# Sheaf pass of a four-layer graph kernel: 40 columns fetched by TensorE from a table in four float32r tiles, 12 gathered by GpSimd

## The chip, the core and the metric

One core of one Trainium2 chip. The metric is the device time of one execution in microseconds (us). Engines by their names in the profile: PE is TensorE (PEld its weight loads), DVE is VectorE, ACT is ScalarE, POOL is GpSimd, SP is SyncE.

## The reference

Four graph layers run one after the other over the same graph of N = 12500 nodes and 412500 edges (sorted by destination): attention, relations, sheaf, typed attention. The change touches the sheaf layer alone:

```python
xs, xd = (x[src], x[dst])                       # 16 values for each end of each edge
def reflection(a, b):
    h = relu(concatenate([a, b], axis=1) @ W1.T + b1)
    return h @ W2.T + b2
def householder(v):
    vn = v / maximum(norm(v, axis=1, keepdims=True), 1e-12)
    return eye(d)[None] - 2.0 * vn[:, :, None] * vn[:, None, :]
F_s = householder(reflection(xs, xd)); F_d = householder(reflection(xd, xs))
L_sd = -einsum('eki,ekj->eij', F_s, F_d)
coef = deg_inv_sqrt[src] * deg_inv_sqrt[dst]
msg_s = coef[:, None] * einsum('eij,ej->ei', L_sd, xd)
msg_d = coef[:, None] * einsum('eji,ej->ei', L_sd, xs)
out = relu(x - zeros.at[src].add(msg_s) - zeros.at[dst].add(msg_d))
```

## The kernel before, in words

`sheaf_pass` walks the edges in 62 chunks. A chunk is 52 columns (`J`) of 128 edges, one edge per partition. For each edge it needs the row of its source node: 16 values and the inverse root of the degree, `W` = 17 numbers.

**Two ways to fetch a row.** For the first `SJP` = 16 columns POOL gathers rows from DRAM with one indirect DMA per column (line 2097). For the other `SPE` = 36 columns PE fetches them from a table in SBUF. The node's tile number t (0 to 97) is cut into a low part (t mod 7) and a high part (14 values). DVE builds, for four columns at a time, seven one-hot matrices in bfloat16 (`build_low`, line 2164: seven comparisons of 512 elements). PE multiplies each with the table part of that low value (17 x 14 = 238 columns); the table is held as three bfloat16 parts whose sum is the float32 value, so a column of edges costs 7 x 3 = 21 matmuls that add up in PSUM (`find`, line 2352, two columns at a time, 42 matmuls). DVE then multiplies the 2 x 238 results with a one-hot of the high part (line 2183) and sums over the high part (line 2187); the two are `take`. The one-hot of the high part is made once per chunk (`spread_high`, line 2170).

**The chunk's pipeline.** Every engine runs a `turn` per chunk, of `SN` = 18 steps. In step n of the turn of chunk a:
- PE does `find` of step n for the next chunk, then for chunk a `spin` (a transpose, line 2363, steps 3 to 15), `hide` (first layer of the small network, line 2372, steps 4 to 16), `unhide` (second layer, line 2382, steps 5 to 17), and in steps 9 to 12 `add_alike` for the chunk before a (line 2394: sums over edges with the same source).
- DVE does `take` of step n-1 for the next chunk; in even steps `build_low` for a later group; in step 0 `begin` (lines 2207 to 2218: fills in the destination's values, joins the ends) and `spread_high`; in steps 1 to 7 `reflect`, and in step 8 `sum_by_dst` for the chunk before; in step 14 `find_places` (ends with line 2289, which releases POOL's scatters); from step 9 `compare` (line 2229) and from step 6 `take_v` (line 2222). The last `take_v` of a turn stands after step 17.
- ACT copies and bends between PE's steps, and copies the sums of `add_alike` out (`take_added`, line 2449).

`find` of step n waits for `take` of step n-2 (two result buffers in PSUM) and for the one-hots; `take` waits for `find`; `unhide` waits for the `take_v` before it. So PE and DVE keep pace within a step or two.

**POOL** does for each chunk 52 scatters with addition into DRAM (line 2113), each waiting for the one four before it, and between them (after every third) the gathers for the chunk three further on. A chunk's scatters wait for line 2289 of that chunk; halfway through, it frees the buffer of the chunk before, on which ACT's `take_added` of the chunk after waits. PE, DVE and POOL loop over pairs of chunks; DVE's loop starts at line 2326.

**SP** issues the loads: index, the low parts (line 2073, one buffer per chunk parity), high parts, and edge data. PSUM: `found` has two buffers of one bank each; the transposes, `hidden`, `v`, `added` and a mixed bank take one each.

## Time and profile before

| | us |
|---|---|
| median of 3 runs (27705.8 to 27721.6) | 27713.97 |
| profiled execution, its own time | 27723.67 |
| its span | 27721.6 |
| sheaf pass: first `find` to last scatter | 15751 to 23652 |

| engine | busy us of the whole span | share |
|---|---|---|
| PE | 22581.0 | 81% |
| PEld | 17103.5 | 62% |
| DVE | 19269.3 | 70% |
| ACT | 1534.2 | 6% |
| POOL | 17285.6 | 62% |

A busy share is an average over stages with different limits, and only about 7900 us of the span belong to the changed pass. What matters there is which engine goes without a rest, and, where two engines hand work to each other in steps, which of them ends each step. The idle time of an engine is listed with what ended it.

### The profile page before, as it was taken

The numbers are of one execution on the slowest core, as the hardware profiler recorded it, in microseconds if no ns is written. First come the engines' busy times: TensorE is split into PE (matmuls) and PEld (weight loads), VectorE is DVE, ScalarE is ACT, GpSimd is POOL, SyncE is SP. The second block draws the span as 40 slices with busy tenths as digits, with TensorE's granted clock in tenths as the row PEclk, the third lists the DMA queues.
The fourth block names the chain that finished last, engine by engine and source line by source line (L and its number), as shares of the span: only waits on it lengthen the run. The fifth ranks groups of instructions, "written<-read, shape, count | busy, mean of one in ns | idle before, by whom it ended". The sixth has DMA issues, their size and how long they took to land. (4 is left out here: it accounts for less than half of the span.)

```text
span 27721.6 us, 477560 instructions
## 1 busy us (share of the span) xinstructions
PE 22581.0 (81%) x178452; PEld 17103.5 (62%) x178452; DVE 19269.3 (70%) x45474; ACT 1534.2 (6%) x3291; POOL 17285.6 (62%) x15844
## 2 busy tenths in 40 slices
PE   0788876888857999969999398889898897399996
PEld 0444433444426888858888388888888886155554
DVE  4788885555555777757777376676766765499996
ACT  0000000000000000000000011111111111100000
POOL 1555556666654555546655478888888888455555
PEclk9998987999977999979999699999999998599998
DMA  4222221111111111111111122222222222522221
GB/s 80 61 65 63 62 59 28 40 40 40 40 34 32 33 34 34 34 29 32 32 32 31 19 37 39 35 39 37 37 39 35 39 40 25 132 57 60 60 60 42
DMA packets 1658941, 1225.33 MB, mean 44 GB/s; under 512 B 1258202, under 2 KB 1501076, under 8 KB 1615348
## 3 DMA queue, kind: packets, MB, share of 16 engines
q0 software_dynamic: 870816, 181.33, 10.7%
q1 hardware_dynamic: 676628, 585.00, 7.7%
q10 hardware_dynamic: 110016, 437.07, 4.0%
q8 instruction: 1197, 19.61, 0.3%
q14 instruction: 284, 2.33, 0.0%
HBM read 736.61 MB, written 465.15 MB: 43 GB/s over the span
## 5 line engine op out<-in xcount | busy, mean ns | idle before, releaser
L946 PE MATMUL gat_e_found<-gat_e_parts,gat_e_lowhot 128*128 128x400 bf16 (+1 forms) x30504 | 5867.6, 356 | 1077.8 <-DVE gat_e_rows L915 927.4
L2352 PE MATMUL sheaf_e_found<-sheaf_e_parts,sheaf_e_lowhot 128*128 128x238 bf16 x46872 | 5274.5, 274 | 939.5 <-DVE sheaf_e_lowhot L2164 462.4
L2113 POOL DMA_INDIRECT bysrc<-sheaf_e_toadd,sheaf_e_torow x3224 | 5162.4, 1601 | 1312.5 <-issue 758.2
L1027 POOL DMA_INDIRECT gat_e_rows<-att_t,gat_e_index x4464 | 4236.5, 949 | 2676.6 <-DMA gat_e_rows<-att_t,gat_e_index 1423.3
L2352 PEld LDWEIGHTS sheaf_e_found<-sheaf_e_parts,sheaf_e_lowhot 128*128 128x128 bf16 x46872 | 4688.9, 101 | 1370.0 <-issue 546.2
L750 POOL DMA_INDIRECT rgcn_e_rows<-rel_t,rgcn_e_index x3968 | 3753.8, 946 | 2844.5 <-DMA rgcn_e_rows<-rel_t,rgcn_e_index 1468.4
L946 PEld LDWEIGHTS gat_e_found<-gat_e_parts,gat_e_lowhot 128*128 128x128 bf16 x30504 | 3035.1, 100 | 3909.7 <-DVE gat_e_rows L915 996.3
L1843 PEld LDWEIGHTS rgcn_e_found<-rgcn_e_parts,rgcn_e_lowhot 128*128 128x128 bf16 x52080 | 5033.8, 99 | 559.4 <-issue 490.5
L1843 PE MATMUL rgcn_e_found<-rgcn_e_parts,rgcn_e_lowhot 128*128 128x224 bf16 x52080 | 5245.8, 264 | 78.9 <-issue 72.0
L2801 POOL DMA_INDIRECT typed_e_rows<-typed_t,typed_e_index x1984 | 1903.4, 959 | 1434.7 <-DMA typed_e_rows<-typed_t,typed_e_index 910.5
L946 PE MATMUL typed_e_found<-typed_e_parts,typed_e_lowhot 128*128 128x400 bf16 x14880 | 2686.0, 338 | 57.9 <-DVE typed_e_lowhot L890 57.9
L946 PEld LDWEIGHTS typed_e_found<-typed_e_parts,typed_e_lowhot 128*128 128x128 bf16 x14880 | 1477.8, 99 | 1093.4 <-issue 131.6
L2183 DVE TENSOR_TENSOR sheaf_e_picked<-sheaf_e_found,sheaf_e_highhot 128x476 f32<-128x476 f32 x1116 | 723.7, 648 | 1956.3 <-PE sheaf_e_found L2352 1855.8
L910 DVE TENSOR_TENSOR gat_e_picked<-gat_e_found,gat_e_highhot 128x800 f32<-128x800 f32 (+1 forms) x992 | 1011.4, 1020 | 774.4 <-PE gat_e_found L946 767.6
L1719 DVE TENSOR_TENSOR rgcn_e_bykind<-rgcn_e_kindsp,rgcn_e_hot 128x512 f32<-128x512 f32 x620 | 427.3, 689 | 1374.6 <-PE rgcn_e_kindsp L1863 1373.7
L2097 POOL DMA_INDIRECT sheaf_e_rows<-sheaf_t,sheaf_e_index x992 | 1074.7, 1083 | 390.2 <-issue 290.5
L1696 DVE TENSOR_SCALAR rgcn_e_lowhot<-rgcn_e_low,whole_lowf 128x512 bf16<-128x512 f16 x4340 | 1306.7, 370 | 0.3
L2164 DVE TENSOR_SCALAR sheaf_e_lowhot<-sheaf_e_low,whole_lowf 128x512 bf16<-128x512 f16 x3906 | 1192.8, 375 | 0.3 <-DVE sheaf_e_parts L826 0.2
L699 DVE TENSOR_TENSOR_SCAN gat_e_sums<-gat_e_miscp,gat_e_sums,gat_e_scaled 128x52 f32<-128x52 f32 x4960 | 1134.8, 301 | 0.0
L915 DVE TENSOR_REDUCE gat_e_rows<-gat_e_picked 128x32 f32<-128x800 f32 (+1 forms) x992 | 1026.4, 1035 | 34.0
L2382 PE MATMUL sheaf_e_vp<-sheaf_w,sheaf_e_hidden 128*128 128x32 f32 x6448 | 828.0, 274 | 235.8 <-DVE sheaf_e_v L2222 232.8
L2382 PEld LDWEIGHTS sheaf_e_vp<-sheaf_w,sheaf_e_hidden 128*128 128x128 f32 x6448 | 815.2, 199 | 255.9 <-issue 240.5
(497 smaller groups left out, 22017.0 us busy)
## 6 DMA issues: line engine op xcount, KB each, us to landing
sheaf_e_allsrc<-src_d ACTq DMA_DIRECT2D x62, 1664.0 KB
sumsatt<-gat_e_sums ACTq DMA_DIRECT2D x62, 1404.0 KB
rgcn_e_low<-low_d SPq DMA_DIRECT2D x124, 640.0 KB
typed_e_types<-in_type_t SPq DMA_DIRECT2D x62, 1280.0 KB, 8.1
typed_t<-typed_p_y SPq DMA_DIRECT2D x98, 765.0 KB
gat_e_rows<-att_t,gat_e_index POOLq DMA_INDIRECT x4464
sheaf_e_low<-low_d SPq DMA_DIRECT2D x62, 1152.0 KB
sumsatt<-gat_e_sums ACTq DMA_DIRECT2D x62, 1092.0 KB
```

The lines of the kernel that those rows point to most:

```text
L699: return dve.tensor_tensor_scan(out, keep, values, before, ALU.mult, ALU.add)
L750: pool.indirect_dma_start(self.rows[k][:, j, :], None, table, rows(self.index[k][:, j:j + 1]))\
L946: last = pe.matmul(self.found_ps[n % 2][:, c, 0:self.width * self.cut.highs], hot[:, k, col * P:(col + 1) * P], self.table.column(part, k) ...
L1027: pool.indirect_dma_start(rows_t[a.k][:, j, :], None, table, rows(index[a.k][:, j:j + 1]))\
L1696: last = dve.tensor_scalar(low_hot[(k * NQ + q) % 2][:, n, :], low[k][:, q * QC * P:(q + 1) * QC * P], g.low_f[:, n:n + 1], None, ALU.is_e ...
L1843: last = pe.matmul(found_ps[at % 2][:, c, 0:NHI * FD], low_hot[at % 2][:, n, c * P:(c + 1) * P], short.column(part, n), start=n == 0 and p ...
L2097: pool.indirect_dma_start(rows_t[a.k][:, j, :], None, table, rows(index[a.k][:, j:j + 1]))\
L2113: pool.indirect_dma_start(g.by_src[k][r], rows(to_row[k][:, j:j + 1]), to_add[k][:, j, 0:FD], None, compute_op=ALU.add).then_inc(summed[k] ...
L2164: last = dve.tensor_scalar(hot[:, n, :], low[a.k][:, q * QC * P:(q + 1) * QC * P], g.low_f[:, n:n + 1], None, ALU.is_equal)
L2352: last = pe.matmul(found_ps[n % 2][:, c, 0:W * NHI], hot[:, k, col * P:(col + 1) * P], short.column(part, k), start=part == 0 and k == 0, ...
L2382: last = pe.matmul(v_ps[:, c * F2:(c + 1) * F2], hidden[(a.k * NQ13 + m) % 2][:, c * P:(c + 1) * P], w2, start=True, stop=True)
L2801: pool.indirect_dma_start(rows_t[a.k][:, j, :], None, table, rows(index[a.k][:, j:j + 1]))\
```

## The change

TensorE's share of the columns goes from 36 to 40, and GpSimd's gathers from 16 to 12 per chunk. The tile number is cut by 4 instead of 7: four low values, and 25 high values made up to 26, so a table part is 17 x 26 = 442 columns wide. The table is held in two float32r parts instead of three bfloat16 ones, so a column of edges is 4 x 2 = 8 matmuls; the one-hots of the low part become float32r, those of the high part bfloat16. A turn has 20 steps instead of 18. `found` takes two banks per buffer; to make room `ends` and `added` share a bank, with waits that keep PE's writes and ACT's reads apart, and `add_alike` moves to steps 10 to 13 and ahead of `find`. The last `take_v` comes in step 18. `find_places` moves to step 15. The low parts are loaded in halves of a chunk. The 52 comparisons are spread over 11 steps instead of 9.

```diff
-SPE = 36
+SPE = 40
 SJP = J - SPE
 SG = SPE // QC
 SN = 2 * SG
 NQ13 = J // QC
-CUTS = (0, 12, 24, 36, J)
+PART = J // 4
+CUTS = tuple(range(0, J + 1, PART))
...
+    cut_by = Cut(FLO, FHI + FHI % 2, g.few_low_d, g.few_high_d, 2, F32R)
+    tiles, highs = cut_by.tiles, cut_by.highs
...
-        low = [s.sb(f"low{k}", [P, SPE * P], F16) for k in range(2)]
+        low = [s.sb(f"low{k}", [P, SPE * P // 2], F16) for k in range(2)]
...
-        short = SplitTable(s, sevenths(g), [values[:, :, :]], W, same[0][:, :, :].rearrange("p j q -> p (j q)").bitcast(F32))
-        low_hot = [s.sb(f"lowhot{k}", [P, NLO, QC * P], BF16) for k in range(2)]
-        high_hot = [s.sb(f"highhot{k}", [P, SPE, NHI]) for k in range(2)]
-        picked = s.sb("picked", [P, 2, W, NHI])
+        short = SplitTable(s, cut_by, [values[:, :, :]], W, same[0][:, :, :].rearrange("p j q -> p (j q)").bitcast(F32))
+        low_hot = [s.sb(f"lowhot{k}", [P, tiles, QC * P], cut_by.exact) for k in range(2)]
+        high_hot = [s.sb(f"highhot{k}", [P, SPE, highs], BF16) for k in range(2)]
+        picked = s.sb("picked", [P, 2, W, highs])
...
-        found_ps = [s.ps(f"found{k}", [P, 2, 256]) for k in range(2)]
-        ends_ps, hidden_ps, v_ps = s.ps("endsp", [P, P]), s.ps("hiddenp", [P, QC * P]), s.ps("vp", [P, QC * F2])
-        added_ps, misc_ps = s.ps("addedp", [P, 16, MW]), s.ps("miscp", [P, 512])
+        found_ps = [s.ps(f"found{k}", [P, 2, 512]) for k in range(2)]
+        hidden_ps, v_ps, misc_ps = s.ps("hiddenp", [P, QC * P]), s.ps("vp", [P, QC * F2]), s.ps("miscp", [P, 512])
+        shared_ps = s.ps("sharedp", [P, 512])
+        ends_ps, added_ps = shared_ps[:, 0:P], shared_ps[:, P:P + PART * MW].rearrange("p (j c) -> p j c", c=MW)
...
+                def load_low(a, half, fresh):
+
+                    if not fresh:
+                        sp.wait_ge(low_built, a.c * SG - (SG // 2 if half == 0 else 0))
+                    lo = SJP + half * (SPE // 2)
+                    sp.dma_start(low[half][:, :], line(low_v, a.c, lo * P, (lo + SPE // 2) * P))\
+                        .then_inc(low_in[half], 16)
...
-                    if not fresh:
-                        sp.wait_ge(low_built, (c - 1) * SG)
-                    sp.dma_start(low[k][:, :], line(low_v, c, SJP * P, J * P)).then_inc(low_in[k], 16)
+                    load_low(a, 0, fresh and k == 0)
                     if not fresh:
                         sp.wait_ge(high_built, c - 1)
-                    sp.dma_start(high_in[k][:, :], chunk(g.high_d, i, k)[:, SJP:]).then_inc(high_in_s[k], 16)
+                    sp.dma_start(high_in[k][:, :], chunk(cut_by.high_d, i, k)[:, SJP:]).then_inc(high_in_s[k], 16)
...
+                    load_low(a, 1, fresh and k == 0)
...
-                    if q == 0:
-                        dve.wait_ge(low_in[a.k], a.turn * 16 + 16)
+                    half, at = q // (SG // 2), q % (SG // 2)
+                    if at == 0:
+                        dve.wait_ge(low_in[half], a.c * 16 + 16)
                     if not fresh:
                         dve.wait_ge(found, 2 * (a.c * SG + q) - 2)
                     hot = low_hot[(a.k * SG + q) % 2]
-                    for n in range(NLO):
-                        last = dve.tensor_scalar(hot[:, n, :], low[a.k][:, q * QC * P:(q + 1) * QC * P],
+                    for n in range(tiles):
+                        last = dve.tensor_scalar(hot[:, n, :], low[half][:, at * QC * P:(at + 1) * QC * P],
                                                  g.low_f[:, n:n + 1], None, ALU.is_equal)
...
-                                             g.count_f[:, 0:NHI].unsqueeze(1).to_broadcast([P, SPE, NHI]),
-                                             high_in[a.k][:, :].unsqueeze(2).to_broadcast([P, SPE, NHI]),
+                                             g.count_f[:, 0:highs].unsqueeze(1).to_broadcast([P, SPE, highs]),
+                                             high_in[a.k][:, :].unsqueeze(2).to_broadcast([P, SPE, highs]),
...
-                                             found_ps[n % 2][:, :, 0:W * NHI].rearrange("p c (f h) -> p c f h", f=W),
+                                             found_ps[n % 2][:, :, 0:W * highs].rearrange("p c (f h) -> p c f h", f=W),
                                              high_hot[a.k][:, 2 * n:2 * n + 2, :].unsqueeze(2)
-                                             .to_broadcast([P, 2, W, NHI]), ALU.mult))
+                                             .to_broadcast([P, 2, W, highs]), ALU.mult))
...
-                        if reflects and n == 14:
+                        if reflects and n == 15:
                             find_places(o, old)
                         if moves and n >= 9:
-                            compare(o, a, range((n - 9) * 6, min(J, (n - 8) * 6)))
-                        if moves and n >= 6:
+                            compare(o, a, range((n - 9) * J // (SN - 9), (n - 8) * J // (SN - 9)))
+                        if moves and 6 <= n < 6 + NQ13:
                             take_v(a, n - 6)
-                    if moves:
-                        take_v(a, NQ13 - 1)
...
-                        for part in range(3):
-                            for k in range(NLO):
-                                last = pe.matmul(found_ps[n % 2][:, c, 0:W * NHI], hot[:, k, col * P:(col + 1) * P],
+                        for part in range(cut_by.pieces):
+                            for k in range(tiles):
+                                last = pe.matmul(found_ps[n % 2][:, c, 0:W * highs], hot[:, k, col * P:(col + 1) * P],
                                                  short.column(part, k), start=part == 0 and k == 0,
-                                                 stop=part == 2 and k == NLO - 1)
+                                                 stop=part == cut_by.pieces - 1 and k == tiles - 1)
...
+                def spin(a, m, first=False, beside=False, added_before=None):
                     M = a.c * NQ13 + m
                     if m == 0:
                         pe.wait_ge(ends_ready, a.c + 1)
                     if not (first and m == 0):
                         pe.wait_ge(ends_copied, M)
+                    if beside:
+                        pe.wait_ge(added_out, added_before)
...
-                def add_alike(a, part, first=False):
+                def add_alike(a, part, copied, first=False):
+                    pe.wait_ge(ends_copied, copied)
...
+                        adds = reflects and 10 <= n <= 13
+                        if adds:
+                            copied = a.c * NQ13 + n - 3 if moves else a.c * NQ13
+                            add_alike(old, n - 10, copied, first=isinstance(old.turn, int) and old.c == 0)
                         if fetches:
                             find(nxt, n)
                         if moves and 3 <= n <= 15:
-                            spin(a, n - 3, first)
+                            spin(a, n - 3, first, adds, old.c * 4 + n - 9)
                         if moves and 4 <= n <= 16:
                             hide(a, n - 4, first)
                         if moves and 5 <= n <= 17:
                             unhide(a, n - 5, first)
-                        if reflects and 9 <= n <= 12:
-                            add_alike(old, n - 9, first=isinstance(old.turn, int) and old.c == 0)
...
+                        if reflects and 10 <= n <= 13:
+                            take_added(old, n - 10)
```

`Cut(tiles, highs, low_d, high_d, pieces, exact)` only holds its arguments. `g.few_low_d` and `g.few_high_d` exist already; they are those of the attention layers' cut by four.

## Rows read from the trace of the kernel before

**Rows 1.** Groups in 16370 to 22250 us: engine, tiles, count; busy, mean ns; idle, releasers.
```profile
L2352 PE MATMUL sheaf_e_found<-sheaf_e_parts,sheaf_e_lowhot 128*128 128x238 bf16 x35892 | 4044.2, 274 | 412.3 <-DVE sheaf_e_rows L2187 330.5 <-issue 54.0 <-DVE sheaf_e_lowhot L2164 27.2
L2113 POOL DMA_INDIRECT bysrc<-sheaf_e_toadd,sheaf_e_torow x2465 | 3944.4, 1600 | 879.6 <-issue 573.6 <-DMA bysrc<-sheaf_e_toadd,sheaf_e_torow 302.8 <-DVE sheaf_e_torow L2289 3.3
...
L2164 DVE TENSOR_SCALAR sheaf_e_lowhot<-sheaf_e_low,whole_lowf 128x512 bf16<-128x512 f16 x2996 | 916.8, 375 | 0.0
...
L2187 DVE TENSOR_REDUCE sheaf_e_rows<-sheaf_e_picked 128x34 f32<-128x476 f32 x855 | 554.8, 649 | 29.4
L2183 DVE TENSOR_TENSOR sheaf_e_picked<-sheaf_e_found,sheaf_e_highhot 128x476 f32<-128x476 f32 x855 | 554.4, 648 | 1499.3 <-PE sheaf_e_found L2352 1408.8 <-issue 50.2 <-DVE sheaf_e_highhot L2170 11.6
```

**Rows 2.** The same stretch, busy time of each engine and TensorE's granted clock.
```profile
core 0: us, PE busy (x) PEld busy (x) DVE busy (x) ACT busy (x) POOL busy (x), PEclk, DMA share, GB/s
16370.00:22250.00 5880.00, 5293.14 (x53910) 4941.19 (x53908) 4071.46 (x10747) 850.46 (x1618) 4769.22 (x3223) 0.96 0.29 37
```

**Rows 3.** Timeline of POOL in mid-pass: start, duration, instruction, idle before.
```profile
18018.22 1.55 POOL L2113 DMA_INDIRECT bysrc<-sheaf_e_toadd,sheaf_e_torow  x1 [0.30 <-issue]
18020.07 1.01 POOL L2097 DMA_INDIRECT sheaf_e_rows<-sheaf_t,sheaf_e_index  x1 [0.30 <-issue]
18021.39 1.57 POOL L2113 DMA_INDIRECT bysrc<-sheaf_e_toadd,sheaf_e_torow  x1 [0.30 <-DMA bysrc<-sheaf_e_toadd,sheaf_e_torow]
```

**Rows 4.** Instructions of lines 2289 and 2113: duration, first and last start.
```profile
L2289 DVE TENSOR_SCALAR sheaf_e_torow<-sheaf_e_place,sheaf_e_spare x62: 248/249/450, 16035.5 to 23510.0; 128x52 int32<-128x52 f32 x62
...
L2113 POOL DMA_INDIRECT bysrc<-sheaf_e_toadd,sheaf_e_torow x3224: 1549/1552/3262, 16036.6 to 23650.2; - x190
```

**Rows 5.** Timeline of PE: a step of the turn, with `add_alike`.
```profile
18240.46 4.50 PE L2352 MATMUL sheaf_e_found<-sheaf_e_parts,sheaf_e_lowhot 128*128 128x238 bf16 x42
18244.80 0.27 PE L2363 MATMUL sheaf_e_endsp<-whole_ident,sheaf_e_ends 128*128 128x128 f32 x1
18244.91 1.06 PE L2372 MATMUL sheaf_e_hiddenp<-sheaf_e_endst,sheaf_w 128*128 128x128 f32 x8
18245.80 0.98 PE L2382 MATMUL sheaf_e_vp<-sheaf_w,sheaf_e_hidden 128*128 128x32 f32 x8
18246.61 1.05 PE L2394 MATMUL sheaf_e_addedp<-sheaf_e_piece,sheaf_e_same 128*128 128x18 bf16 x36
18247.52 4.51 PE L2352 MATMUL sheaf_e_found<-sheaf_e_parts,sheaf_e_lowhot 128*128 128x238 bf16 x42
```

**Rows 6.** Timeline of DVE: turn end, step 0, steps 7 and 8.
```profile
18166.23 0.29 DVE L2222 TENSOR_TENSOR sheaf_e_v<-sheaf_e_vp,sheaf_b 128x128 f32<-128x128 f32 x1 [4.22 <-PE sheaf_e_vp L2382]
18171.09 0.65 DVE L2183 TENSOR_TENSOR sheaf_e_picked<-sheaf_e_found,sheaf_e_highhot 128x476 f32<-128x476 f32 x1 [4.57 <-PE sheaf_e_found L2352]
...
18217.65 0.64 DVE L2183 TENSOR_TENSOR sheaf_e_picked<-sheaf_e_found,sheaf_e_highhot 128x476 f32<-128x476 f32 x1
...
18224.94 0.65 DVE L2183 TENSOR_TENSOR sheaf_e_picked<-sheaf_e_found,sheaf_e_highhot 128x476 f32<-128x476 f32 x1 [4.52 <-PE sheaf_e_found L2352]
...
18232.27 0.64 DVE L2183 TENSOR_TENSOR sheaf_e_picked<-sheaf_e_found,sheaf_e_highhot 128x476 f32<-128x476 f32 x1
```

**Rows 7.** Timeline of PE in step 7: after a wait of 3.35 us.
```profile
18217.88 1.05 PE L2382 MATMUL sheaf_e_vp<-sheaf_w,sheaf_e_hidden 128*128 128x32 f32 x8 [3.35 <-DVE sheaf_e_v L2222]
18218.76 6.14 PE L2352 MATMUL sheaf_e_found<-sheaf_e_parts,sheaf_e_lowhot 128*128 128x238 bf16 x42
```

**Rows 8.** Timeline of PE, typed pass: a `find` 400 columns wide.
```profile
25006.08 4.22 PE L946 MATMUL typed_e_found<-typed_e_parts,typed_e_lowhot 128*128 128x400 bf16 x24
```

**Rows 9.** Groups of the whole span with other widths and types.
```profile
L1863 PE MATMUL rgcn_e_kindsp<-rgcn_ws,rgcn_e_hcol 64*128 64x512 f32 x1240 | 752.7, 689 | 1.9 <-DVE rgcn_e_bykind L1719 1.9
...
L915 DVE TENSOR_REDUCE typed_e_hrows<-typed_e_picked 128x32 f32<-128x800 f32 x620 | 611.3, 986 | 21.1
L910 DVE TENSOR_TENSOR typed_e_picked<-typed_e_found,typed_e_highhot 128x800 f32<-128x800 f32 x620 | 609.2, 983 | 243.9 <-PE typed_e_found L946 209.6 <-DVE typed_e_scaled L2844 14.2 <-DVE typed_e_attr L2827 12.8
...
L2710 DVE TENSOR_SCALAR typed_e_typehot<-typed_e_types,whole_lanef 128x512 bf16<-128x512 int32 x310 | 155.9, 503 | 0.3
...
L826 DVE CAST sheaf_e_parts<-sheaf_e_same 128x238 bf16<-128x238 f32 x21 | 14.2, 678 | 0.3
```

More of the change, by code:

```diff
@@ L24 @@
 BF16 = mybir.dt.bfloat16
+F32R = mybir.dt.float32r
 F16 = mybir.dt.float16
@@ L2054, in sheaf_pass @@
         acc = by_edge(sums_d)
-        low_v, all_v = (t.rearrange("(c m) -> c m", m=J * P) for t in (g.low_d, g.src16_d))
+        low_v, all_v = (t.rearrange("(c m) -> c m", m=J * P) for t in (cut_by.low_d, g.src16_d))
         per_table = J // NSUM
@@ L2324, in _ @@
                 turn(o, At(1, 0))
-                base, per = o.n, 2 * 44
+                base, per = o.n, 2 * (SN + 26)
                 with dve.Fori(1, NCH // 2 - 2) as i:
@@ L2349, in find @@
                         col = (n % 2) * 2 + c
-                        for part in range(3):
-                            for k in range(NLO):
-                                last = pe.matmul(found_ps[n % 2][:, c, 0:W * NHI], hot[:, k, col * P:(col + 1) * P],
+                        for part in range(cut_by.pieces):
+                            for k in range(tiles):
+                                last = pe.matmul(found_ps[n % 2][:, c, 0:W * highs], hot[:, k, col * P:(col + 1) * P],
                                                  short.column(part, k), start=part == 0 and k == 0,
-                                                 stop=part == 2 and k == NLO - 1)
+                                                 stop=part == cut_by.pieces - 1 and k == tiles - 1)
                     last.then_inc(found, 1)
-                def spin(a, m, first=False):
+                def spin(a, m, first=False, beside=False, added_before=None):
                     M = a.c * NQ13 + m
@@ L2470, in turn @@
                                 .then_inc(stored[old.k], 16)
-                        if reflects and 9 <= n <= 12:
-                            take_added(old, n - 9)
                 turn(At(0, 0), reflects=False, first=True)
```

## The prediction

> **What bounds the kernel now.** I read the pass in this order: the groups of its steady middle, POOL's timeline, the first and last starts of the two lines that hand POOL its work, and then one turn on PE and on DVE step by step.
>
> *POOL does not rest.* In 5880 us it issues 2465 scatters, 47.4 chunks' worth: 124.0 us per chunk. Its idle time is almost all "issue" and its own earlier scatters; line 2289, which releases it, ends 3.3 us of it [rows 1]. A scatter takes 1.85 us from start to start and a gather 1.32 [rows 3], so 52 and 16 of them would take 96.2 + 21.1 = 117.3 us; the other 6.7 are longer ones (mean 1600 ns where most take 1552) and waits for earlier scatters [rows 1, 4].
>
> *PE and DVE are no faster.* The first scatter starts 1.1 us after the first run of line 2289. The last chunk's 52 scatters must start at 23650.2 - 51 x 1.85 = 23555.9, 46 us after its line 2289 at 23510.0 [rows 4]. So in 61 chunks the pair gained only 46 us on POOL; half of that I count to the last turns, which have few or no finds (an estimate). The pair's own period is within a microsecond of POOL's.
>
> *Who ends which step.* With `add_alike` a PE step is 7.06 us: find 4.34, transpose 0.11, hide 0.89, unhide 0.81, sums 0.91; without, 6.15 [rows 5]. PE sets steps 10 to 16: four with sums (one has 48 matmuls of sums instead of 36, 0.3 longer) and three without, 47.2 us. DVE sets steps 0 to 6: from the `take` at 18171.09 to the one at 18217.65 it goes through 46.6 us of its own work. Step 7 is 7.3 us, in which DVE waits 4.52 for a `find`, and step 8 is 7.3, DVE's own [rows 6]. What remains of 124.0 for step 9 and the turn's end is 15.6; it holds a 4.57 us gap on DVE where its loop starts anew, in every second chunk [rows 6], 2.3 on average. The row puts that gap down to PE; I take it for the loop's own.
>
> **The change, part by part, per chunk.**
>
> *Matmuls of a find.* 42 of 238 columns become 16 of 442. A bfloat16 find of 24 matmuls of 400 columns takes 4.22 less its last one's tail of 0.16: 0.169 each [rows 5, 8], so 0.187 for 442 if float32r streams a column as fast as bfloat16 does, 2.99 us instead of 4.34. The trace has no float32r. The other end is float32: 0.689 us for 512 columns as a mean with its tail, or 752.7/1240 = 0.607 without, twice per product [rows 9], 0.52 for 442. I take the low end: `hide` issues four float32 matmuls and eight run [rows 5], so a float32 product is split in two, and float32r is one; and the row nearest in width and pattern is the 400-column one. PE per chunk: 20 x 2.99 + 13 x 1.81 + 4 x 0.99 = 87 us instead of 18 x 4.34 + 23.5 + 3.9 = 106. Both ends are kept as cases.
>
> *Weight loads.* They now carry four bytes. The 32-column float32 matmuls run at 0.81/8 = 0.101 us, which can only be their weight loads; the 128-column ones at 0.89/8 = 0.111 [rows 5]. Loads in series with the streaming would show as more than 0.2. So they hide under 0.187 us, at no cost; unhidden they would be 16 x 0.101 = 1.6 us per find, the other end. The Trainium skill ("TensorE: Matmul & The Clock Gate", Weight-path perf modes) speaks against this change: it has the fast weight load on for 128 weights only where their type is not FP32. By that rule, the trace agrees: 36 bfloat16 loads and matmuls pass in 0.91 us, 0.025 each, a quarter of 0.101 [rows 5].
>
> *Low one-hots.* 9 groups of 7 comparisons become 10 of 4, written as four bytes. One costs 916.8/2996 = 0.306 us start to start. With a four-byte operand on one side, the same 512 elements have a mean of 503 ns against 375 [rows 1, 9]: 0.434 each, 1.74 us a group instead of 2.14, if DVE keeps its two elements per cycle. The other end is one element per cycle, 0.27 more each (the 128 ns step from four to two is a quarter of 512 cycles, so the next is half), 2.8 a group. I take 1.74: the int32 row is a comparison of the same length with one four-byte side.
>
> *Take.* 2 x 17 x 26 = 884 elements instead of 476. Both halves cost 648 ns now, and at 800 elements 983 and 986 [rows 1, 9], 1.04 ns per element; so 1.07 each, +0.85 us per take, and 20 instead of 18. `spread_high` handles 1040 elements instead of 504, +0.55. DVE in all: 4071/47.4 = 86 us per chunk now [rows 2], less 9 x 2.14 and 18 x 1.30, plus 10 x 1.74, 20 x 2.14 and 0.55: 104.
>
> *The turn.* Steps 0 to 6 hold seven takes and four groups: 46.6 + 6.0 - 1.6 + 0.55 = 51.5. Step 7 waits for unhide and find; that find now takes 1.64 us longer than one of 4.50 [rows 5], after PE had waited 3.35 [rows 7]. I carry the 1.64 over: 1.1 + 2.99 + 1.64 + 0.15 = 5.9. Step 8: 7.3 + 0.85 - 0.4 = 7.8. Steps 10 to 13 are PE's, 4.80 + 0.99 = 5.8 each, 23.2. Steps 14 to 18: PE 4.8, DVE 4.9 and 3.2 in turn, so 4.8 each, 24.0. Step 9 and the end, now steps 9 and 19: a find that may start cold, 5.0, and DVE's 3.3 + 2.3 of loop, since no `take_v` waits there any more: 10.6. Sum 123.0 against 124.0. PE's 19 us are given back by two more steps and by the seven takes that stand where DVE sets the pace.
>
> *POOL.* Four gathers less: 117.3 - 5.3 + 6.7 = 118.7 us. It would wait for line 2289 some 4 us per chunk. *SP.* The low halves are issued behind waits for one-hots already built; half 1 stands behind the wait for `same_ready` and is wanted eight steps later, some 50 us, and the next index load, which queues behind it, is wanted by POOL only 15 steps on. Nothing. *New waits.* `spin` waits for ACT's copy of the sums (0.36 us work), with the 3 us find between; behind it queue hide and unhide. Nothing while the find covers it, otherwise 4 x 0.5 us. *Ends.* The table costs 8 casts instead of 21 (14.2 us now [rows 9]), at most 442/238 as long, and 4 subtractions instead of 14: -8. The first chunk's finds run alone: 18 x 4.34 = 78 against DVE's 20 x 2.15 + 10 x 1.74 = 60: -18. POOL no longer trails by what it had lost up to the last two turns: -23.
>
> *Sum.* 60 x -1.0 - 8 - 18 - 23 = -109 us. The profiled execution took 27723.67 (span 27721.6), 10 above the median of the runs, 27713.97. So 27615 in its terms and 27605 in the median's; I say 27610, 0.4% faster. Its own range, with 1.5 us per chunk either way: 27520 to 27700.
>
> **Rivals.**
>
> 1. *POOL bounds* (faster). PE and DVE overlap better than my steps, and the pass runs at POOL's 118.7: -5.3 x 60 - 49 = -367: 27360 (with 118.7 as its period). For it: DVE's 104 us and PE's 87 are both below. Against: they take turns at setting the pace, and DVE's 51.5 in steps 0 to 6 has no slack.
> 2. *The comparison into float32r runs at one element per cycle* (slower). +1.07 us a group. Five groups stand in steps DVE sets, +5.3; the other five bring DVE's pairs of steps from 8.1 to 9.2 against PE's 9.6, +1.5 by hand-over. +6.8 x 60 = +410: 28020. It decides from +1.8 us per chunk, a comparison of 0.50 instead of 0.43 us. For it: no row writes four bytes from two. Against: the int32 row.
> 3. *float32r streams at half bfloat16's rate* (slower). A find is 5.9 us, PE sets every step: 20 x 5.9 + 27.4 = 145.6, with hand-over 150: +26 x 62 = 29300; at the float32 row's 0.52, past 31000. For it: nothing but the lack of a row.
> 4. *PE drops to half clock in the steps DVE sets* or its weight loads are not hidden (slower). PE would be busy 4.8 of some 7 us there instead of 6.15 of 6.7. At 1.2 GHz a find of 6.0 and 3.6 of the rest make 9.6 against DVE's 6.8, six times: +17 per chunk, 28600. The granted clock is 0.96 of 2.4 GHz now [rows 2], and a find after a wait loses 1.64 us, not half its speed throughout [rows 7]. The Trainium skill (same page, The HAM clock gate) has TensorE at 1.2 GHz when it was idle and at 2.4 after sustained work; by that rule, the trace agrees. Unhidden loads would make nine steps 1.6 longer: +14, 28500.
> 5. *The change doesn't do what it says*: the pass keeps 124 us because something outside my steps (a load of the halves, the shared bank) holds each turn for a microsecond or more. That lies within the forecast's range and above it up to 27800.
>
> **How the numbers follow.** Forecast 0.60, POOL bounds 0.07, half-rate comparison 0.12, slow float32r 0.10, clock or loads 0.07, rival 5 0.04. About 0.2% (55 us) is what a measurement of this kernel can tell from no change. Of the forecast's 0.60, with its 1.5 us per chunk, 0.38 lie below 27659, 0.14 within and 0.08 above: faster 0.45, same 0.17, slower 0.38 with the others. The range runs from the POOL-bound case to the half-rate comparison, 27360 to 28110; it leaves out rivals 3 and 4.
>
> **What would show it.** The float32r matmul's spacing is 0.187 us (0.37: rival 3). The comparison's mean is about 500 ns (770: rival 2), each half of `take` 1070. POOL's scatters have idle time ended by line 2289, several us per chunk (none: rival 1). DVE's idle time before the multiplication of `take` falls from 1499.3 us in the middle [rows 1] to about half. PE waits mostly for line 2187 in steps 0 to 6. The prediction is wrong if the period is below 120 or above 125.

## The result: 0.9% slower

The changed kernel takes 27963.07 us (median, 27955.9 to 27980.1), the kernel before 27717.78 in the same runs: ratio 1.009, 95% interval 1.0073 to 1.0107. The span of the profiled execution is 27965.9 us, 244.3 more than before.

The same stretch of the pass after the change, 16370 to 22250 us, by groups (columns as in [rows 1]); then the tile view of POOL's scatters and of line 2302, which releases them (it was line 2289 before; minimum, median and longest ns, first and last start):

```profile
L2125 POOL DMA_INDIRECT bysrc<-sheaf_e_toadd,sheaf_e_torow x2390 | 3933.6, 1646 | 1199.8 <-issue 1062.3 <-DMA bysrc<-sheaf_e_toadd,sheaf_e_torow 137.5
L2363 PE MATMUL sheaf_e_found<-sheaf_e_parts,sheaf_e_lowhot 128*128 128x442 f32 x14704 | 3618.0, 406 | 787.3 <-DVE sheaf_e_rows L2200 782.4 <-issue 4.6
L2200 DVE TENSOR_REDUCE sheaf_e_rows<-sheaf_e_picked 128x34 f32<-128x884 f32 x920 | 988.0, 1074 | 31.7
L2196 DVE TENSOR_TENSOR sheaf_e_picked<-sheaf_e_found,sheaf_e_highhot 128x884 f32<-128x884 f32 x920 | 987.5, 1073 | 986.9 <-PE sheaf_e_found L2363 863.7 <-issue 75.0 <-DVE sheaf_e_highhot L2183 14.7
L2177 DVE TENSOR_SCALAR sheaf_e_lowhot<-sheaf_e_low,whole_lowf 128x512 fp32r<-128x512 f16 x1840 | 816.5, 505 | 0.0
L2395 PE MATMUL sheaf_e_vp<-sheaf_w,sheaf_e_hidden 128*128 128x32 f32 x4784 | 618.1, 274 | 261.6 <-DVE sheaf_e_v L2235 261.6
```

```profile
L2125 POOL DMA_INDIRECT bysrc<-sheaf_e_toadd,sheaf_e_torow x3224: 1549/1552/3007, 15999.2 to 23838.2; - x190
L2302 DVE TENSOR_SCALAR sheaf_e_torow<-sheaf_e_place,sheaf_e_spare x62: 248/249/251, 15998.0 to 23698.1; 128x52 int32<-128x52 f32 x62
```

POOL issues 2390 scatters in 5880 us instead of 2465: 127.9 us per chunk against 124.0 [rows 1]. Its idle time rose from 879.6 to 1199.8 us: it now waits for the pair of PE and DVE. The view calls this time "issue", but the starts show it: in all but the last two chunks the first scatter starts 0.9 to 1.3 us after line 2302 ends, while before POOL had fallen 24 us behind by the third chunk from the end. The DVE prices of the prediction are met: each half of `take` 1073 ns (1070 predicted), a comparison 505 ns (500), DVE in all 4795/45.96 = 104.3 us per chunk (104). On PE, the wait of `unhide` for `take_v` (line 2235) has grown from 171.6 us, 3.6 per chunk, to 261.6, 5.7 per chunk. The kernel before has, in the same stretch:

```profile
L2382 PE MATMUL sheaf_e_vp<-sheaf_w,sheaf_e_hidden 128*128 128x32 f32 x4960 | 627.7, 271 | 174.6 <-DVE sheaf_e_v L2222 171.6 <-ACT sheaf_e_hidden L2436 2.9
```

By stretches (columns as in [rows 2]):

```profile
16370.00:22250.00 5880.00, 4831.12 (x32014) 4460.37 (x32013) 4794.83 (x9516) 823.38 (x1562) 4512.85 (x2942) 0.89 0.28 36
...
17951.00:18000.00 49.00, 37.07 (x167) 33.54 (x168) 43.74 (x51) 6.63 (x12) 41.07 (x27) 0.79 0.23 19
18013.00:18055.00 42.00, 42.00 (x368) 39.96 (x365) 30.03 (x80) 7.83 (x17) 25.31 (x17) 1.00 0.17 5
```

The granted clock fell from 0.96 to 0.89 of 2.4 GHz over the pass; in this turn it is 1.00 where PE sets the pace (steps 10 to 17) and 0.79, a mean, where DVE does (steps 1 to 7). There TensorE goes back and forth between 1.2 and 2.4 GHz; a `find` at full clock takes 3.50 us, and the one at 17991.05 below 5.34.

One turn, PE in steps 6 to 10 (the timeline's columns as in [rows 5]):

```profile
17985.01 1.06 PE L2385 MATMUL sheaf_e_hiddenp<-sheaf_e_endst,sheaf_w 128*128 128x128 f32 x8
17989.35 1.89 PE L2395 MATMUL sheaf_e_vp<-sheaf_w,sheaf_e_hidden 128*128 128x32 f32 x8 [3.29 <-DVE sheaf_e_v L2235]
17991.05 5.34 PE L2363 MATMUL sheaf_e_found<-sheaf_e_parts,sheaf_e_lowhot 128*128 128x442 f32 x16
...
18001.49 1.06 PE L2385 MATMUL sheaf_e_hiddenp<-sheaf_e_endst,sheaf_w 128*128 128x128 f32 x8
18004.44 1.05 PE L2395 MATMUL sheaf_e_vp<-sheaf_w,sheaf_e_hidden 128*128 128x32 f32 x8 [1.89 <-DVE sheaf_e_v L2235]
18005.33 5.03 PE L2363 MATMUL sheaf_e_found<-sheaf_e_parts,sheaf_e_lowhot 128*128 128x442 f32 x16
...
18013.00 3.50 PE L2363 MATMUL sheaf_e_found<-sheaf_e_parts,sheaf_e_lowhot 128*128 128x442 f32 x16
```

and DVE in the same steps:

```profile
17988.92 0.29 DVE L2235 TENSOR_TENSOR sheaf_e_v<-sheaf_e_vp,sheaf_b 128x128 f32<-128x128 f32 x1 [0.24 <-DVE sheaf_e_twice L2280]
17989.13 1.07 DVE L2196 TENSOR_TENSOR sheaf_e_picked<-sheaf_e_found,sheaf_e_highhot 128x884 f32<-128x884 f32 x1
...
17996.43 1.08 DVE L2196 TENSOR_TENSOR sheaf_e_picked<-sheaf_e_found,sheaf_e_highhot 128x884 f32<-128x884 f32 x1 [3.68 <-PE sheaf_e_found L2363]
...
18000.22 3.57 DVE L700 TENSOR_TENSOR_SCAN sheaf_e_sums<-sheaf_e_miscp,sheaf_e_sums,sheaf_e_twice 128x52 f32<-128x52 f32 x16
18004.01 0.29 DVE L2235 TENSOR_TENSOR sheaf_e_v<-sheaf_e_vp,sheaf_b 128x128 f32<-128x128 f32 x1 [0.23 <-DVE sheaf_e_sums L700]
...
18010.40 1.08 DVE L2196 TENSOR_TENSOR sheaf_e_picked<-sheaf_e_found,sheaf_e_highhot 128x884 f32<-128x884 f32 x1 [3.05 <-PE sheaf_e_found L2363]
```

This is the loss to read. `take_v` stands at the end of DVE's step, behind `reflect` or `sum_by_dst`. PE is done with `hide` at 17986.1 and stands; the `take_v` at 17988.92 lets it go. The `unhide` and the `find` behind it then run at half clock for a while (1.70 instead of 0.81 us, 5.34 instead of 3.50), and DVE, done with its own work, waits 3.68 us for that find. The same again two steps on.

Start to start of `take` in us, by steps of the turn, mean of 44 chunks of the middle. The prediction's sum stands first; the kernels of the last three columns come from the experiments below:

| steps | predicted | changed kernel | take_v early | repeats in 6 and 8 | last version |
|---|---|---|---|---|---|
| 0 to 6 | 51.5 | 51.9 | 51.7 | 51.9 | 47.5 |
| 7 | 5.9 | 6.8 | 3.6 | 4.7 | 3.6 |
| 8 | 7.8 | 7.8 | 7.9 | 7.8 | 7.9 |
| 10 to 13 | 23.2 | 24.5 | 24.0 | 24.5 | 25.6 |
| 14 to 18 | 24.0 | 25.3 | 25.3 | 25.3 | 25.4 |
| 9 and 19 | 10.6 | 11.6 | 8.3 | 10.1 | 8.3 |
| sum | 123.0 | 127.9 | 120.7 | 124.2 | 118.3 |

By the same mean the kernel before takes 123.7 us for its 18 steps. The 124.0 of [rows 1] is POOL's, which fell behind the pair by a fraction of a microsecond per chunk.

### The profile page after: what moved, and what is told of

Its sections match the earlier page's. It is cut to its first block and busy times, and to the rows that moved or that the text cites. A ratio compares the mean times of both kernels' runs of the same rounds, so it can differ in the third digit from the quotient of the medians.

```text
span 27965.9 us, 423023 instructions
## 1 busy us (share of the span) xinstructions
PE 22165.5 (79%) x151420; PEld 16657.4 (60%) x151420; DVE 20388.2 (73%) x44274; ACT 1536.8 (5%) x3291; POOL 17116.6 (61%) x15596
## 3 DMA queue, kind: packets, MB, share of 16 engines
q0 software_dynamic: 862880, 179.15, 10.6%
## 5 line engine op out<-in xcount | busy, mean ns | idle before, releaser
L2125 POOL DMA_INDIRECT bysrc<-sheaf_e_toadd,sheaf_e_torow x3224 | 5295.9, 1643 | 1765.7 <-issue 1392.0
L2363 PE MATMUL sheaf_e_found<-sheaf_e_parts,sheaf_e_lowhot 128*128 128x442 f32 x19840 | 4856.7, 404 | 1445.9 <-DVE sheaf_e_rows L2200 1021.0
L2363 PEld LDWEIGHTS sheaf_e_found<-sheaf_e_parts,sheaf_e_lowhot 128*128 128x128 f32 x19840 | 4145.0, 214 | 1859.3 <-DVE sheaf_e_rows L2200 1087.5
L2196 DVE TENSOR_TENSOR sheaf_e_picked<-sheaf_e_found,sheaf_e_highhot 128x884 f32<-128x884 f32 x1240 | 1331.1, 1073 | 1314.8 <-PE sheaf_e_found L2363 1164.7
L2200 DVE TENSOR_REDUCE sheaf_e_rows<-sheaf_e_picked 128x34 f32<-128x884 f32 x1240 | 1331.7, 1074 | 42.7
L2177 DVE TENSOR_SCALAR sheaf_e_lowhot<-sheaf_e_low,whole_lowf 128x512 fp32r<-128x512 f16 x2480 | 1097.7, 504 | 0.3
```

The source lines that it names most:

```text
L2125: pool.indirect_dma_start(g.by_src[k][r], rows(to_row[k][:, j:j + 1]), to_add[k][:, j, 0:FD], None, compute_op=ALU.add).then_inc(summed[k] ...
L2196: o.link(dve.tensor_tensor(picked[:, :, :, :], found_ps[n % 2][:, :, 0:W * highs].rearrange("p c (f h) -> p c f h", f=W), high_hot[a.k][:, ...
L2200: dve.tensor_reduce(rows_t[a.k][:, SJP + 2 * n:SJP + 2 * n + 2, :], picked[:, :, :, :], AX.X, ALU.add).then_inc(taken, 1)
L2363: last = pe.matmul(found_ps[n % 2][:, c, 0:W * highs], hot[:, k, col * P:(col + 1) * P], short.column(part, k), start=part == 0 and k == 0 ...
```

## The experiments

**take_v early.** `take_v` goes right behind `take` in each step (cuts of the edit are marked with "...", here and below):

```diff
 def fetch(..., then=None):
     take(...)
+    if then is not None: then()      # take_v(a, n - 6) in steps 6 to 18
     if n % 2 == 0: build_low(...)
...
-                        if moves and 6 <= n < 6 + NQ13:
-                            take_v(a, n - 6)
```

> The changed kernel with one edit: in every step of VectorE's turn, take_v stands right behind take, ahead of the low one-hots, reflect and sum_by_dst. Theory A (late take_v): in the changed kernel PE stops at unhide in steps 6 and 8 (3.29 and 1.89 us in one turn) for a take_v that stands at the end of DVE's step, so the next find starts late and cold, and DVE then waits 3.68 us in step 7 and 3.05 us in step 9 for it. With take_v early both waits go: 128.0 us per chunk become 121 to 122.5, 27963 - 60 x 6 = 27600 us (27550 to 27650). Theory B (DVE's larger take is the bound, 104 us of work per chunk with no slack): the order of the work inside a step changes nothing, 27930 to 27990. Theory C (only the clock costs): the waits shorten but the finds in steps 7 and 9 stay at 4.6 us, so about 3 us per chunk of the 6 are had, 27780.

The result is 27552.7 us, ratio to the kernel before 0.9929 (0.9912 to 0.9945). Steps 7 and 9 are 3.2 us shorter each, and little else moved. Its PE and DVE in steps 6 and 7:

```profile
18013.43 1.05 PE L2398 MATMUL sheaf_e_vp<-sheaf_w,sheaf_e_hidden 128*128 128x32 f32 x8 [0.46 <-DVE sheaf_e_v L2237]
18014.31 3.48 PE L2366 MATMUL sheaf_e_found<-sheaf_e_parts,sheaf_e_lowhot 128*128 128x442 f32 x16
```

```profile
18016.46 1.08 DVE L2196 TENSOR_TENSOR sheaf_e_picked<-sheaf_e_found,sheaf_e_highhot 128x884 f32<-128x884 f32 x1 [0.24 <-DVE sheaf_e_twice L2282]
...
18020.01 1.08 DVE L2196 TENSOR_TENSOR sheaf_e_picked<-sheaf_e_found,sheaf_e_highhot 128x884 f32<-128x884 f32 x1 [0.24 <-DVE sheaf_e_twice L2282]
```

The wait is 0.46 us, the find runs at full clock, and DVE waits for it no more. `take` is as large as before this edit and the kernel is faster than the one before the change, so the larger `take` is not what made it slower.

**Repeats, wait kept.** To part the clock from the wait, PE was kept busy with matmuls that compute the same result again:

```diff
-                    for c in range(QC):
+                    for c in list(range(QC)) * (3 if m in (1, 2, 3, 4) else 1):   # in hide
```

> The changed kernel, take_v where it was, but hide issues its matmuls three times over (the same result) for groups 1 to 4, in PE's steps 5 to 8, where PE stands waiting; 1.8 us more of PE work in each. It keeps TensorE busy without taking any wait away. Theory C (the clock is what costs): the finds of steps 7 and 9 fall from 4.6 to 3.13 us, DVE's waits in steps 7 and 9 fall by 1.5 each, 128.0 becomes 125 us per chunk, 27963 - 180 = 27780. Theory A alone (the place of take_v, clock a minor part): the finds get at most half of that back and where ACT's bend comes later than take_v a little is lost: 27900 to 27980. Theory B: 27963, no change.

The result is 27982.1 us, ratio 1.0084 (1.0067 to 1.0101): no gain. Three rounds did not fill the wait of step 6: in one turn `unhide` still waited 3.05 us there, and the find of step 7 took 5.42. The find of step 9 ran at full clock (3.49 us, where the changed kernel has 4.97), but PE has no wait in step 7 and a short one in step 8, and there the repeats delayed the finds by about what the clock gave. So the repeats were put only where PE waits: four rounds in step 6 (m = 2) and three in step 8 (m = 4).

> The changed kernel, take_v where it was; hide issues its matmuls four times in PE's step 6 and three times in step 8, and once elsewhere, so that the repeats (2.7 and 1.8 us) fill the two waits for take_v (3.29 and 1.89 us in the trace) and lengthen no step. It takes away only TensorE's idleness. In the run with three repeats in steps 5 to 8 the find of step 9 ran at full clock (3.1 us instead of 4.6) but steps 7 and 8 had paid 1.8 us for it. Clock theory: finds of steps 7 and 9 at 3.1 to 3.3 us, the turn shorter by 1.6 + 1.5, 124.9 us per chunk, 27963 - 186 = 27780. If PE falls to half clock there for another reason than its idleness: 27960.

The result is 27768.9 us, ratio 1.0008 (0.9998 to 1.0017), a gain of 0.8% on the changed kernel by matmuls that compute nothing new. Steps 6 and 8 on PE:

```profile
17961.22 3.74 PE L2386 MATMUL sheaf_e_hiddenp<-sheaf_e_endst,sheaf_w 128*128 128x128 f32 x32
17965.57 1.05 PE L2396 MATMUL sheaf_e_vp<-sheaf_w,sheaf_e_hidden 128*128 128x32 f32 x8 [0.61 <-DVE sheaf_e_v L2236]
17966.45 3.50 PE L2364 MATMUL sheaf_e_found<-sheaf_e_parts,sheaf_e_lowhot 128*128 128x442 f32 x16
...
17975.03 2.84 PE L2386 MATMUL sheaf_e_hiddenp<-sheaf_e_endst,sheaf_w 128*128 128x128 f32 x24
...
17978.90 3.50 PE L2364 MATMUL sheaf_e_found<-sheaf_e_parts,sheaf_e_lowhot 128*128 128x442 f32 x16
```

Both finds run at full clock, though `take_v` comes no earlier in DVE's step than before. The clock alone is worth 3.7 us per chunk, half of the 7.2 that the early `take_v` has; the rest is the wait itself.

**The parts of the table.** The use of float32r undone, with the four tiles kept:

```diff
-    cut_by = Cut(FLO, FHI + FHI % 2, g.few_low_d, g.few_high_d, 2, F32R)
+    cut_by = quarters(g)     # Cut(FLO, FHI, g.few_low_d, g.few_high_d, 3, BF16)
```

> The changed kernel with the float32r part undone: the same four tiles, in three bfloat16 parts, 425 columns wide: 24 matmuls per find instead of 16. At 0.177 + 0.003 each a find is 4.3 us instead of 3.34, a group of low one-hots 1.2 us instead of 1.7. Steps 10 to 18, set by PE, grow by 0.95 each, 8.5 us; steps 7 and 9 by 1 each; steps 0 to 6, DVE's, lose 2.5. 128.0 becomes 135.5 per chunk: 28410 us (28250 to 28500). If DVE's load set the pace in all steps it would be below 27963.

The result is 28469.9 us, ratio 1.0263 (1.0243 to 1.0284). In the next kernel 12 of the 16 matmuls of a find leave out the last 102 of the 442 columns:

```diff
+    wide = W * highs if (part, k) in ((0, 0), (cut_by.pieces - 1, tiles - 1)) else 340
-    last = pe.matmul(found_ps[n % 2][:, c, 0:W * highs], ..., short.column(part, k), ...)
+    last = pe.matmul(found_ps[n % 2][:, c, 0:wide], ..., short.column(part, k)[:, 0:wide], ...)
```

> Leaves out part of the products: 12 of the 16 matmuls of a find read only 340 of the 442 table columns (the first and the last of each column of edges keep all 442). It measures what paces a float32r matmul, which has a spacing of 0.203 us at full clock where 0.187 was predicted. If the columns pace it with a fixed 0.019 on top, the narrow ones have 340/442 of 0.184 and the 0.019: 0.161 us. If the weight load (0.19 in the trace) paces it, they stay at 0.195 to 0.205 and the kernel's time stays within 20 us of 27963. With the first, finds in PE-set steps fall by 12 x 0.042 = 0.5 us, the chunk by 9 x 0.5 = 4.5, less where DVE then sets the step: 27700 to 27800.

The result is 27633.2 us, ratio 0.9958 (0.9942 to 0.9974). A find at full clock in the one and in the other:

```profile
18021.67 4.54 PE L2363 MATMUL sheaf_e_found<-sheaf_e_parts,sheaf_e_lowhot 128*128 128x425 bf16 x24
```

```profile
18032.51 2.94 PE L2365 MATMUL sheaf_e_found<-sheaf_e_parts,sheaf_e_lowhot 128*128 128x442 f32 x16
```

Less the tail of 0.16, bfloat16 is 0.1825 us for 425 columns. The changed kernel's float32r is 3.34/16 = 0.209 for 442. Narrowed, 2.78 = 4 x 0.209 + 12 x 0.162. The single records of the traces say the same from start to start inside a find: 0.203 for 442 columns and 0.157 for 340; the rest of the 0.209 is one longer step, 0.285, behind a find's first matmul. So the columns pace float32r too (102 fewer take 0.046 off), and not the weight load. But at 2.4 GHz 442 columns are 0.184 us and 425 are 0.177: a float32r matmul has nearly 0.02 on top, the bfloat16 one 0.005. Why is open. With the hand-over it costs 0.35 us per find, and in steps 10 to 17, which PE sets, it is paid in full; step 18 measures the 4.8 us that was predicted. Float32r is still right: with bfloat16 these steps are a microsecond longer.

**The split undone.** The table of the change kept:

```diff
-SPE = 40
+SPE = 36
...
-                    half, at = q // (SG // 2), q % (SG // 2)
+                    half, at = (0, q) if q < 5 else (1, q - 5)      # and the loads in 5 and 4 groups
...
+                    if moves:
+                        take_v(a, NQ13 - 1)      # after the last step, as before the change
```

> The changed kernel with the split undone: TensorE fetches 36 columns and GpSimd gathers 16, in 18 steps, with the float32r table of four tiles kept. If my account of the steps is right, PE and DVE lose two steps of about 5.1 us and need 118 us per chunk, and POOL, at its 124.0 of before, sets the pass: 27700 to 27740, the same as before within 0.2%. If instead POOL was not the bound of the kernel before (the pair alone set 124), it comes near 118 + hand-over: 27400 to 27500. If the float32r finds and the wider take cost more than they give even with 36 columns: above 27800.

The result is 27629.4 us, ratio 0.9945 (0.9928 to 0.9962), 123.1 us per chunk. It lies between the two expectations: POOL does set the pace (its scatters trail line 2302 by 29 us or more from the tenth chunk on, so it never waits for the pair), but at 123.1 instead of 124.0. DVE waits for POOL's gathers in its step 0 (total us, times, longest); the kernel before and the changed one have no such line:

```profile
DVE sheaf_e_ends L2228 <- DMA sheaf_e_rows<-sheaf_t,sheaf_e_index: 83.7, 28, 3.8
```

So at 36 columns the new table alone was a gain of 0.5%, and in the changed kernel's order of work the four moved columns cost 336 us by the spans, 288 of them in the pass (60 x 4.8) and most of the rest in the typed pass (below).

**The kernel before, take_v early.** The same edit there:

> The kernel before (36 columns by TensorE, seven bfloat16 tiles) with take_v right behind take in DVE's steps. If POOL's work was the bound of the kernel before, as its 16 gathers at 123.1 us per chunk in the run with the split undone say, the pair gains about 3 us in step 7 and nothing of it is had but 0.8 us per chunk: 27670 to 27750, same. If the pair of PE and DVE set the pace alone, 3 us x 60: 27570.

The result is 27607.8 us, ratio 0.9952 (0.9935 to 0.9968), 121.9 us per chunk: a larger gain than the POOL account allowed, a smaller one than the pair's. ACT waits for POOL to free a buffer (no such line before), and POOL's scatters trail line 2289 by 37 us, so POOL bounds it, at 121.9:

```profile
ACT sheaf_e_toadd L2452 <- POOLq L2122: 391.7, 45, 9.5
```

POOL's floor with 16 gathers is therefore not the 124.0 that I had read from [rows 1]. With hardly a wait for the pair, the same 52 scatters and 16 gathers took 124.0 us in the kernel before, 123.1 with the split undone and 121.9 here; of that, waits for its own earlier scatters were 6.6, 4.9 and 3.9 us per chunk. What makes these waits differ is open. The pair alone needed 123.7 in the kernel before. Between the two kernels with `take_v` early, the change is worth 120.7 against 121.9 us per chunk, and by the whole time 0.9929/0.9952, some 0.2% faster; the two intervals overlap, so the whole time alone does not show it.

**DVE's work moved.** From the kernel with `take_v` early: the 17 scans of `begin` go to steps 14 to 17 of the turn before, `spread_high` of the chunk after to step 18.

```diff
+                        if fetches and 14 <= n <= 17:
+                            fill(o, nxt, (n - 14) * W // 4, (n - 13) * W // 4)
+                        if fetches and not last and n == 18:
+                            spread_high(o, nxt.next())
```

> The changed kernel with take_v early, and DVE work moved out of step 0, where DVE sets the pace, into steps where PE sets it: the 17 scans that fill in the destination's values for the next chunk go to steps 14 to 17, spread_high of the chunk after goes to step 18. 5.5 us leave step 0 (11.1 in the run with take_v early); DVE's five steps 14 to 18 grow from 20.2 to 25.6 us against PE's 25.1, so about 1 us comes back. The pair would need 116.5 us per chunk; POOL's floor with 12 gathers is 123.1 - 5.3 = 117.8. So POOL sets the pass at 118: 27553 - 60 x 2.7 = 27390 (27360 to 27440), and its first scatter of a chunk starts later and later after line 2302. If DVE's work fits nowhere (DVE bounds at 104 us plus waits): 27500 to 27600.

The result is 27420.7 us, ratio 0.9884 (0.9868 to 0.9901), 118.6 us per chunk. Step 0 fell from 11.1 to 7.0, steps 14 to 18 grew from 25.3 to 27.0.

**Instructions in other places.** One thing was still unexplained: the typed pass, untouched, had become 56 us longer. `take`'s multiplication there, before and after:

```profile
L910 DVE TENSOR_TENSOR typed_e_picked<-typed_e_found,typed_e_highhot x620: 961/991/993, 24222.5 to 27538.5; 128x800 f32<-128x800 f32 x155
```

```profile
L911 DVE TENSOR_TENSOR typed_e_picked<-typed_e_found,typed_e_highhot x620: 960/991/993, 24410.3 to 27782.6; 128x800 f32<-128x800 f32 x155
```

From first to last start that is 3316.0 against 3372.3 us. The edit adds waits that are long satisfied, 60 or 20 of them, behind DVE's last turn of the sheaf pass. In the traces they are 30 and 10 more instructions of DVE:

```diff
+                for _ in range(60):
+                    dve.wait_ge(taken, 1)
```

> The changed kernel with 60 waits on a semaphore that is long satisfied (30 instructions of DVE) put behind DVE's last turn of the sheaf pass. They do nothing but move DVE's instructions of the typed pass to other places in the program; the typed pass itself isn't edited. Seen so far: the typed pass, untouched by the change, takes 3372 us from first to last take in the changed kernel and 3316 in the one before, because after its loop's branch DVE stands 3.1 us in every second chunk where it stood 0.23; the same in all runs with 40 columns, and not in the run with 36. The Trainium skill (Runtime: NRT & Kernel Launch, Instruction fetch mechanics) has instructions fetched in blocks of 256, two of which are held, and a stall on a branch to one outside. Place theory: a loop of 310 instructions fits two blocks or not by where it begins; with 30 more it begins 8 into a block and fits: the stall falls to 0.25 us, the typed pass to 3316 us, the kernel to 27963 - 56 = 27907. If the 56 us come from what the pass leaves behind (buffers, queues): no change, 27963.

> The same with 20 waits (10 instructions). Place theory: the typed loop still begins over 202 instructions into its block, the stall stays at 3.1 us and the typed pass at 3372 us, the kernel at 27963. If any added instruction, or the time they take, removes the stall: 27907.

With 60: 27922.0 us, ratio 1.0074 (1.0057 to 1.0091), the typed pass 3314.4. With 20: 28065.1 us, ratio 1.0122 (1.0101 to 1.0142), the typed pass 3457.6. The ratio for 60 waits can't be told from the changed kernel's 1.009; the typed pass can. DVE where the typed loop begins anew, in the changed kernel, with 60 and with 20:

```profile
26310.87 0.75 DVE L700 TENSOR_TENSOR_SCAN typed_e_sums<-typed_e_miscp,typed_e_sums,typed_e_scaled 128x52 f32<-128x52 f32 x3
26315.26 0.99 DVE L911 TENSOR_TENSOR typed_e_picked<-typed_e_found,typed_e_highhot 128x800 f32<-128x800 f32 x1 [3.63 <-issue]
```

```profile
26261.10 0.99 DVE L911 TENSOR_TENSOR typed_e_picked<-typed_e_found,typed_e_highhot 128x800 f32<-128x800 f32 x1 [0.71 <-PE typed_e_found L947]
```

```profile
26359.58 0.99 DVE L911 TENSOR_TENSOR typed_e_picked<-typed_e_found,typed_e_highhot 128x800 f32<-128x800 f32 x1 [3.71 <-issue]
...
26364.49 0.49 DVE L2728 TENSOR_SCALAR typed_e_typehot<-typed_e_types,whole_lanef 128x512 bf16<-128x512 int32 x1 [2.90 <-issue]
```

The place decides. From the loop's branch to the next instruction DVE stands 3.1 us in the changed kernel and 0.23 in the one before. What ended the idle time before `take` in the typed pass (total us, times), before and in the changed kernel:

```profile
  PE typed_e_found L946: 209.6, 232
```

```profile
  PE typed_e_found L947: 161.1, 184
  issue: 104.3, 29
```

So 104.3 us of standing at the branch are new, and 48.5 us less are spent on waiting for PE's finds, which leaves the 56. By the Trainium skill ("Runtime: NRT & Kernel Launch", Instruction fetch mechanics), a branch to a block outside the two that are held stalls the engine; by that rule, the trace agrees, at 3.1 us. With 20 waits I had expected the old stall alone; there is a second one, 2.90 us, a few instructions behind the branch. The same rule would give it if the loop began just short of a block's end: the branch waits for one block and, a few instructions on, for the next. That the blocks are the reason is inferred; what the runs show is that the place is.

**The last version.** `take_v` early, the scans in steps 10 to 13, `spread_high` in step 17, and the 60 waits:

> The kernel with take_v early and DVE's work moved (scans and spread_high out of step 0), with the scans now in steps 10 to 13, where PE takes 6.1 us and DVE 4.6, and spread_high in step 17, which has no low one-hots; and with the 60 waits. In the first version of it steps 14, 16 and 18 had grown by 0.8, 0.5 and 1.3 us, 2.1 in all over the turn; here these fall away, and the pair would need 116.5 us per chunk. POOL's 12 gathers and 52 scatters then set the pace at 117.5 to 118.3, against 118.6: 27421 - 40 - 56 = 27325 (27290 to 27360). If POOL did not bound, 116.5: 27240. If place theory is wrong, 27380.

The result is 27364.6 us, ratio 0.9864 (0.9845 to 0.9882): 1.4% faster than the kernel before, the fastest version here. It lies 5 us above the range that was expected: 118.3 us per chunk by the table and 118.5 by POOL's scatters, because POOL now sets the pace (they trail `find_places` by some 30 us). Of its list of waits:

```profile
ACT sheaf_e_toadd L2481 <- POOLq L2134: 198.8, 30, 13.2
```

The scans no longer lengthen steps 14 to 18 (25.4), but step 11 waits for POOL's buffer. Its gain on the version before, 56 us, is that of the typed pass.

## Why the prediction was wrong

I said 27610, 0.4% faster; it is 0.9% slower. In the profiled executions the sum was -109 us and the result is +244: 353 apart.

- **The turn, 60 x (127.9 - 123.0) = 294 us of it.** By the table: 0.4 in steps 0 to 6, 2.6 in steps 10 to 18, 0.9 in step 7, 1.0 in steps 9 and 19.
- *The starting point, 60 x 0.3 = 18 us.* I took 124.0 as the pair's period before; it was 123.7, and the pair sets the changed kernel.
- *Matmuls of a find* was mis-sized: 0.187 where 0.209 is measured, 16 x 0.022 = 0.35 us in each of steps 10 to 17 (step 17 has no transpose, and step 18, without `hide` too, took 4.8 as predicted). The bfloat16 width account held to 0.003 (0.1825 against 0.180 for 425); carrying it over to float32r did not.
- *The turn, step 7.* I had seen PE's wait of 3.35 us [rows 7] and carried the find's 1.64 over; 1.66 is measured. But the find is 0.35 longer at full clock too, and `unhide` also runs at half clock: 1.70 instead of 0.81 in the turn shown, 1.40 in the mean of 44 chunks. These 0.35 and 0.6 are the missing 0.9.
- *The turn, step 9.* This is the step of the prediction that failed in its mechanism. I took a find that may start cold, but on time, and put steps 9 and 19 at 10.6; they took 11.6, and 8.3 once `take_v` came early. It cannot start on time: `unhide` waits for the `take_v` behind the 3.57 us of scans in step 8. Before, PE's step of 6.15 covered most of that (0.4 us of wait were left); a find shorter by a microsecond, beside a `take` longer by 0.85, uncovered it. The gain on PE made the wait, and the wait made TensorE slow.
- **Rival 4** has the right mechanism and the wrong size. I had half clock in six steps and 17 us; in the turn shown the finds of steps 1, 2, 4 and 6 do run at half clock, but DVE's work covers them. It costs only where PE is on the path: 3.7 us per chunk, 222 us (the run with repeats in steps 6 and 8). Without that alone, the result is within 0.2% of the kernel before. I gave clock and loads together 0.07.
- **56 us lie outside the pass**, in the typed loop's place in the program. No step of mine looked there.
- What held: `take`, the comparison, `spread_high` (DVE 104.3), step 8, hidden weight loads, and no cost of the loads, the shared bank or the new waits of `spin` (steps 10 to 13 are 4.80 + 0.99 + 0.35). The ends held too. From the first cast of the table to the first end of line 2302 it is 27.6 us shorter, where I had counted 8 + 18, and DVE's last two turns are 23.6 shorter, where I had counted 23. The passes ahead of the changed one ended 10 us earlier in this execution, which no edit explains.
- The whole difference, read from the first and last starts: the first scatter comes 37.4 us earlier, the scatters span 7839.0 us against 7613.6 [rows 4], +225.4, and the typed pass adds 56.3. Together that is the +244.
- POOL's floor of 118.7 with 12 gathers was right in the end (118.5), but by luck, through two errors that cancel: with 16 it was 121.9 and not 124.0, and the four gathers were worth 3.4 us and not 5.3.
- The period of 127.9 is outside the 120 to 125 that I had named as the bounds.

## What to carry to other kernels

When a change makes one of two engines that hand work to each other faster, list every wait of that engine that its length had covered, and ask where in the other's step the releasing instruction stands: moving one small instruction to the front of its step turned 0.9% slower into 0.7% faster. Work taken off a TensorE that waits is partly lost again to its clock, but only in the steps where the other engine waits for it. And a program whose loops have moved can be slower in a part that nobody touched, so compare the unchanged stages too before you blame the changed one.

## What the hardware showed that I had not expected

- A float32r matmul of 442 columns takes 0.203 us from start to start inside a find (0.209 with the find's hand-over), 0.184 for its columns at 2.4 GHz and nearly 0.02 more; bfloat16 with 425 takes 0.1825.
- DVE stands 3.1 us at the typed loop's branch, or 0.23, by where the loop lies among its instructions, and in one place it stood a second time a few instructions on. Ten instructions more made the typed pass 85 us longer, thirty made it 58 shorter.
- The same 52 scatters and 16 gathers take GpSimd 121.9, 123.1 or 124.0 us per chunk in three kernels, each time with hardly a wait for the pair.
- Matmuls that repeat a result, put where TensorE waits anyway, took the kernel from 1.009 to 1.0008 of the one before.
